# Key gathers in flight: four in the second layer, two in the last

## The reference

```
xr = einsum('nd,rdf->rnf', x, W)          # one projection for each relation
oi = xr[etype, dst];  oj = xr[etype, src]
alpha = leaky_relu(oi @ q + oj @ k, 0.2)  # one score for each edge and head
m = segment_max(alpha, dst)
e = exp(alpha - m[dst]);  z = segment_sum(e, dst)
out = segment_sum((e / (z[dst] + 1e-16)) * oj, dst) + b
```

## Time and profile before

| what | value |
|---|---|
| median of 3 runs | 1756.65 us (1753.17 to 1764.15) |
| the profiled execution, its own time | 1749.84 us |
| its span, first to last instruction | 1748.0 us |
| PE busy | 1506.7 us (86%) |
| DVE busy | 926.9 us (53%) |
| POOL busy | 1016.0 us (58%) |
| ACT busy | 220.2 us (13%) |
| mean granted TensorE clock | 0.920 |

### The profile page before, as it was taken

The page is one execution under the profiler, slowest core; times in us unless marked ns, Lnnn a source line. Parts: engine busy times, 40 slices in busy tenths (PEclk is TensorE's granted clock), DMA queues, the critical chain, the costliest instruction groups (busy, mean ns, idle before and its releaser), DMA issues.

```text
span 1748.0 us, 25342 instructions
## 1 busy us (share of the span) xinstructions
PE 1506.7 (86%) x6330; PEld 879.2 (50%) x6330; DVE 926.9 (53%) x2169; ACT 220.2 (13%) x530; POOL 1016.0 (58%) x1112
## 2 busy tenths in 40 slices
PE   5989999989866995999699999864997998899996
PEld 2545555545554553566454455433554655455553
DVE  8576722333434877888677777603533345222322
ACT  1545200000000110011000023320110111000000
POOL 1598266665434767775167777515656662666663
PEclk9988999999966997889799999965998999899999
DMA  8201588888720231111188888720231111888887
GB/s 289 113 19 38 188 265 270 268 297 268 228 66 11 56 101 28 38 37 40 65 265 269 263 257 246 223 71 1 56 109 39 38 47 49 280 263 271 263 260 263
DMA packets 86808, 271.76 MB, mean 155 GB/s; under 512 B 32156, under 2 KB 32531, under 8 KB 86743
## 3 DMA queue, kind: packets, MB, share of 16 engines
q0 software_dynamic: 51072, 199.44, 37.7%
q1 hardware_dynamic: 34807, 65.62, 10.5%
q10 hardware_dynamic: 864, 5.90, 0.9%
HBM read 239.28 MB, written 31.62 MB: 155 GB/s over the span
## 4 chain that ended last, share of the span: by engine, by line
PE 57%; issue 14%; DMA 11%; POOL 8%; DVE 8%; DVEq 1%; ACT 1%; another core or an unknown queue 0%; POOLq 0%; SPq 0%; PEldq 0%; ACTq 0%
PE ps L1293 12%; PE ps L1226 9%; DMA ring<-keys,idxr 8%; PE ps L1253 7%; PE ps L1295 6%; PE ps L1296 6%; POOL ring L488 6%; PE ps L1124 5%; DVE zw L962 2%; PE ps L1167 2%; PE ps L1170 2%; PE ps L1187 2%; PE ps L1045 2%; PE ps L1074 1%; PE ps L1087 1%
## 5 line engine op out<-in xcount | busy, mean ns | idle before, releaser
L1253 PE MATMUL ps<-wreg,hT 128*128 128x384 f32 x1440 | 490.0, 503 | 7.4 <-PEq L1246 6.7
L488 POOL DMA_INDIRECT ring<-keys,idxr x312 | 331.1, 1061 | 220.8 <-DMA ring<-keys,idxr 95.3
L459 POOL DMA_INDIRECT ring<-rows,idxr x304 | 311.5, 1025 | 201.7 <-issue 66.6
L1253 PEld LDWEIGHTS ps<-wreg,hT 128*128 128x128 f32 x1440 | 282.2, 197 | 203.9 <-issue 26.7
L1293 PE MATMUL ps<-ring,zw 128*128 x664 | 229.1, 497 | 22.0 <-issue 14.9
L1226 PE MATMUL ps<-ring,zw 128*128 x664 | 223.9, 493 | 21.4 <-DVE zw L851 12.4
L957 DVE TENSOR_TENSOR hn<-hn,al 128x1024 f32 (+1 forms) x166 | 137.6, 829 | 181.7 <-POOL al L506 139.8
L459 POOL DMA_INDIRECT ring<-rows,idx x152 | 145.7, 958 | 116.2 <-PE ps L1226 65.6
L1293 PEld LDWEIGHTS ps<-ring,zw 128*128 128x128 f32 x664 | 122.5, 191 | 123.0 <-issue 53.5
L1226 PEld LDWEIGHTS ps<-ring,zw 128*128 128x128 f32 x664 | 123.8, 191 | 116.0 <-issue 49.5
L1020 DVE TENSOR_TENSOR ring<-ring,al x166 | 159.3, 959 | 40.0 <-issue 19.8
(11 more groups left out here) (185 smaller groups left out, 1232.5 us busy)
## 6 DMA issues: line engine op xcount, KB each, us to landing
wreg<-in_L_gnn_W SPq DMA_DIRECT2D x11, 2304.0 KB, 9.5
rows<-stage SPq DMA_DIRECT2D x30, 386.0 KB
rows<-stage SPq DMA_DIRECT2D x30, 384.5 KB
stT<-targets_row ACTq DMA_DIRECT2D x6, 960.0 KB
ring<-keys,idxr POOLq DMA_INDIRECT x312
ring<-rows,idxr POOLq DMA_INDIRECT x304
rows<-stT SPq DMA_DIRECT2D x10, 384.0 KB, 2.9
xs<-in_x SPq DMA_DIRECT2D x3, 1152.0 KB, 13.5
```

The costliest lines, as they stand in the source:

```text
L459: nc.gpsimd.indirect_dma_start(ring[:, t % (2 * RING), 0:WIDTH[l]], None, rows[l], bass.IndirectOffsetOnAxis(idx[:, t:t + 1], 0)).then_inc ...
L488: nc.gpsimd.indirect_dma_start(kb[:, n % KSEMS, t % KB, 0:4], None, keys[l], bass.IndirectOffsetOnAxis(idxr[:, t:t + 1], 0)).then_inc(k_in ...
L1253: last = mm(ps[:, 2 * (nt % 2) + h, 0:HALF], hT[:, k, nt * P:(nt + 1) * P], wreg[:, r % 2, k, h * HALF:(h + 1) * HALF], start=(k == 0), st ...
```

## The change

The constant `KFLIGHT` becomes a table by layer, 4 in the second layer (key 1) and 2 in the last (key 2). The second layer gets four semaphores `k_in` in place of two, gather t waits for gather t - 4, and each score waits for four semaphores in place of two. The last layer's program stays as it is.

```diff
-KFLIGHT = 2
-assert KB % KFLIGHT == 0
+KFLIGHT = {1: 4, 2: 2}
+assert all(KB % n == 0 for n in KFLIGHT.values())
...
-        k_in = {l: [sem(f"k_in{l}_{i}") for i in range(KFLIGHT)] for l in (1, 2)}
+        k_in = {l: [sem(f"k_in{l}_{i}") for i in range(KFLIGHT[l])] for l in (1, 2)}
...
+                flight = KFLIGHT[l]
+
                 def ask_keys(n):
 
                     for t in range(n * KB, (n + 1) * KB):
-                        if t >= KFLIGHT:
-                            pool.wait_ge(k_in[l][t % KFLIGHT], 16 * (t // KFLIGHT))
-                        nc.gpsimd.indirect_dma_start(kb[:, n % KSEMS, t % KB, 0:4], None, keys[l], bass.IndirectOffsetOnAxis(idxr[:, t:t + 1], 0)).then_inc(k_in[l][t % KFLIGHT], 16)
+                        if t >= flight:
+                            pool.wait_ge(k_in[l][t % flight], 16 * (t // flight))
+                        nc.gpsimd.indirect_dma_start(kb[:, n % KSEMS, t % KB, 0:4], None, keys[l], bass.IndirectOffsetOnAxis(idxr[:, t:t + 1], 0)).then_inc(k_in[l][t % flight], 16)
 
                 def score(n, slot, lows, looped=False):
 
                     batch = al[:, ds(n * (KB * H), KB * H)]
-                    for s in range(KFLIGHT):
-                        pool.wait_ge(k_in[l][s], n * (16 * KB // KFLIGHT) + 16 * KB // KFLIGHT)
+                    for s in range(flight):
+                        pool.wait_ge(k_in[l][s], n * (16 * KB // flight) + 16 * KB // flight)
...
                     for k in range(KB):
-                        pool.wait_ge(k_in[l][k % KFLIGHT], n * (16 * KB // KFLIGHT) + 16 * (k // KFLIGHT))
+                        pool.wait_ge(k_in[l][k % flight], n * (16 * KB // flight) + 16 * (k // flight))
```

More of the change, by code:

```diff
@@ L525, in _ @@
                     for k in range(KB):
-                        pool.wait_ge(k_in[l][k % KFLIGHT], n * (16 * KB // KFLIGHT) + 16 * (k // KFLIGHT))
+                        pool.wait_ge(k_in[l][k % flight], n * (16 * KB // flight) + 16 * (k // flight))
                         pool.sem_inc(turn, 1)
-                        nc.gpsimd.indirect_dma_start(kb[:, KSURE % KSEMS, k, 0:4], None, keys[l], bass.IndirectOffsetOnAxis(idxk[:, k:k + 1], 0)).then_inc(k_in[l][k % KFLIGHT], 16)
+                        nc.gpsimd.indirect_dma_start(kb[:, KSURE % KSEMS, k, 0:4], None, keys[l], bass.IndirectOffsetOnAxis(idxk[:, k:k + 1], 0)).then_inc(k_in[l][k % flight], 16)
                     score(n, KSURE % KSEMS, m * 2 + KSURE, True)
```

## The result

| | before | changed |
|---|---|---|
| median | 1756.31 us (19 runs, 1750.63 to 1765.67) | 1751.23 us (19 runs, 1743.94 to 1757.59) |
| profiled execution, span | 1748.0 us | 1747.3 us |

The ratio of the times is 0.9966, with a 95% interval of 0.9951 to 0.9981: a gain of 6.0 us (3.3 to 8.6), where 13.4 us were forecast. The median lies inside the stated range; the gain does not come near the forecast one. That was on chips where the kernel before takes 1754 to 1756 us. Later runs met chips where it takes 1663 us, and there the change gives 13.0 us; I call them the slower and the faster chips.

The account below looks back on a forecast made before the run. Late key gathers on POOL were taken to starve DVE, which releases PE, in the second layer's maxima stage. 13.1 us from shorter intervals plus 0.35 before batch 8 gave 13.4 us off 1756.65: 1743.2 us, range 1735 to 1752.

Parts of the forecast that it names:

- What bounds the stage: Second layer's maxima stage: gathers feed scores, scores feed DVE's maxima, these release PE; at most 19.6 us to gain through DVE.
- Part 1: Score-to-score intervals, batches 0 to 6: 19.65 us each with four gathers in flight, 117.9 against 131.0 us, 13.1 us sooner.
- The rival with 20.5 us: POOL stays in DVE's step in every gather and the scores: 1748.3 us; chance 0.17 including gains between 3 and 10 us.
- the one with 16.5 us: Score intervals so short that DVE is never starved again: gain all 19.6 us, time 1737.1 us; chance 0.13.
- Part 3: PE after tile 14: waits some 6.5 us for DVE in place of 18.2, and everything behind moves by 13.1 us.
- Part 4: Added costs: two more semaphore waits per score, counted at nothing; faster 24 gathers ahead of score 0 worth nothing, hidden by query work.
- The sum: Whole kernel: 13.4 us less, median from 1756.65 to 1743.2 us, a gain of 0.8%.
- 1 to 3: Rivals: 1, 16.5 us intervals (0.13); 2, 20.5 us intervals (0.17 with neighbouring gains); 3, landings lengthen, nothing moves, 1756.65 us (0.08).
- The slow one: POOL holds what DVE needs more often, so DVE's pairs grow: 1752.3 us in mild form, up to 1764 us; slow side 0.04.

Follow-up runs that it names:

- nokeys: Changed kernel without any key gathers in the second layer, keys a constant (results not right): ratio 0.979 to the kernel before, median 1711.7 us.
- hold24: Changed kernel, second layer's first 24 gathers kept at two in flight, last layer's same wait made twice: ratio 0.9857 to the kernel before, median 1726.7 us.
- twice_wait_d: Kernel before, each wait of the first 24 gathers made twice in both layers, on a slower chip: ratio 0.9892 to the kernel before, median 1733.2 us.
- pace4: Changed kernel plus three tiny memsets on POOL before each of the second layer's first 24 gathers, faster chip: ratio 0.9913 to the kernel before.
- hold24_l1: Changed kernel with two in flight for the first 24 gathers, in the second layer alone, faster chip: ratio 0.9973 to the kernel before.
- twice_wait: Kernel before, each wait of the first 24 gathers made twice in both layers, on a faster chip: ratio 1.0039 to the kernel before.
- twice_wait_c: Kernel before, each wait of the first 24 gathers made twice in both layers, run again on a faster chip: ratio 1.0045 to the kernel before.
- before_b: The kernel before, unchanged, run again for its profile on a faster chip: span 1662.6 us.
- quarter_d: Changed kernel, second layer's first 24 gathers bringing 32 rows instead of 128, on a slower chip: ratio 1.0001 to the kernel before.

## Why the prediction was wrong

- **What bounds the stage:** right. Gathers, then DVE, then PE, and the most to gain 19.6 us; with no gathers the stage lost 21.0 us. But the first row sum, forecast 13 us sooner, came 2.8 us sooner (874.63 to 871.80).
- **Part 1, the interval:** right in its rule. 19.63 us measured for 19.65, with the steps of 1.52 us. Six intervals are 119.7 us for 117.9. (The steps as listed add up to 16.3 us and not 16.6 for the start of the twelfth gather; with 16.3 the interval is 19.65 us, so nothing changes.) The 131.0 us it was set against is one execution's, and high among them: the same six intervals, with nothing changed in their gathers, take 126.8 to 131.2 us in the six profiles with two in flight, 129.2 in the mean, and 118.2 to 119.7 us in the thirteen with four. So the term of 13.1 us measured 11.3 us in the pair of profiles and about 10 us over all. The rival with 20.5 us and the one with 16.5 us are both out: four in flight does away with the landings, and then DVE's step rules. The Trainium skill's page "SBUF — State Buffer", section "SBUF: two separate sides", says that a VectorE instruction with two SBUF inputs and a GpSimd instruction that reads SBUF lock one shared port pair in turn, each for its whole length. The trace agrees as to the turns that POOL and DVE take (1.21 us a gather, two to a pair), but most scores after a batch, at 0.28 us, escaped the full step.
- **Part 3, what is late next on PE:** wrong in part. I moved PE's work as a block with its lengths of before. The spread behind tile 17 grew from 10.5 to 22.8 us, and PE became the bound of the second half; DVE waited 2.46 us for it. Of the 3.0 us by which the stage fell short (10.4 for 13.4), 1.8 are the intervals and the rest fits this spread. The other profiles put its price near 3 us: with four in flight the stage takes 310.7 to 312.8 us where the spread behind tile 17 takes 22.7 us or more, and 307.4 to 309.4 us on the faster chips, where it takes 8.3 or 8.4 us.
- **Part 4, "the 24 gathers ahead of score 0 get faster too ... worth nothing, and that cover stays":** this is the step that failed. The work that covered them, PE's spread of the queries, was not a fixed length. It runs beside these gathers, and with their step down from 1.36 to 1.25 us it grew from 51.2 to 56.0 us. That is 4.8 us on the path in this pair of profiles, and 5.3 us between the means of the table. On the faster chips the same term was wrong the other way: there the gathers were not covered, and their faster steps were worth 7.2 us. I had named what hides them and not asked whether they hurt it. The trace of before had a sign of it: PE's gaps of "issue" in that spread end 2.8 us after the start of the last gather.
- **The sum:** 13.4 - 3.0 in the stage - 4.8 ahead of it = 5.6 us, for 6.0 measured (3.3 to 8.6). On the faster chips, where PE isn't held up, the change gives 13.0 us for a forecast of 13.4. That is luck in good part, for the split is another: 11.5 in the stage and 7.2 at score 0, which waits for the gathers there, with 3.5 given back behind the stage.
- **Rivals:** 1 to 3 didn't occur. The slow one did in kind, POOL taking from a neighbour, but the neighbour was PE and not DVE: pairs stayed at 3.05 us.

What holds PE up isn't settled. Shown is that it goes away with the gathers (nokeys) and mostly with a wide step of them (hold24, twice_wait_d), that fewer rows don't remove it, that it came in all eight profiles with these gathers on slower chips and in none of the eleven on faster ones, and that the path pays for it. The step itself, the number in flight and how many transfers are open at a time were not varied apart from each other. Every execution timed here was recorded for its profile, so whether recording has a part in it is open too. No version was best on both kinds of chip, though the changed kernel is faster than before on both: hold24 is best on the slower ones (1726.7 us), the changed kernel and pace4 on the faster; hold24 itself was not run there, and hold24_l1 gives up 9 us of the changed kernel's gain.

## What to carry to other kernels

When a change makes one engine's work denser, look at what runs beside it, also where the denser work itself is hidden: a cover has a length, and that length may depend on what it covers. Gaps in the covering work that end with the hidden work or soon after it are the sign, and leaving the hidden work out in one run puts a price on both. Where chips differ by several per cent, forecast and measure on the same kind before a missing gain is put down to the mechanism.

## What the runs showed of the hardware

- On the slower chips, small matmuls of PE (36 in 1.5 us when free) come one to five in 0.7 us or more while POOL issues indirect DMAs at mean steps of 1.17 to 1.40 us; at 1.70 us most of it is gone (spread 37.0 us, 30.6 without gathers). The gaps are dense from the eighth or ninth gather on (517.15 in before, 515.10 in the changed kernel) and end 2.8 to 5.4 us after the start of the last one. On the faster chips the same 17 turns of 36 matmuls took 30.6 us in all eleven profiles, at steps of 1.17 to 1.89 us.
- A second wait on POOL, for what the wait just before it has already seen reached, is not free: the mean step of the gathers was 1.69 us with it (twice_wait_d) against 1.36 us (before), and 1.63 and 1.89 us (twice_wait, twice_wait_c) against 1.36 us (before_b).
- A gather of 32 rows costs POOL 0.86 us (quarter_d), one of 128 rows 0.94 us (before), with DVE idle.
- The same kernel took 1663 us on some chips and 1755 us on others. The row gathers' stages show it as well: from the last layer's first row sum to the end, 234.9 us (before_b) against 258.1 us.
